# A transformer layer on one core: the sixteen transposes of a head's probabilities in one stretch, every other step

## What is computed

```python
q = split_heads(x @ wq + bq)            # 8 heads of 48 features
k = split_heads(x @ wk + bk)
v = split_heads(x @ wv + bv)
scores = jnp.einsum('bhqd,bhkd->bhqk', q, k) * scaling
scores = scores + attn_bias[:, None, :, :]          # adj
attn = jax.nn.softmax(scores, axis=-1)
ctx = jnp.einsum('bhij,bhjd->bhid', attn, v)
ctx = ctx.transpose(0, 2, 1, 3).reshape(b, n, d)
attn_out = ctx @ wo + bo
x = _rmsnorm(x + attn_out, alpha1, gamma1)
ff = jax.nn.silu(x @ w1 + b1) @ w2 + b2
x = _rmsnorm(x + ff, alpha2, gamma2)
# outside: layernorm(x_in + x)
```

## Time and profile before

| | us |
|---|---|
| median of the timed runs | 2019.77 |
| profiled execution, its own time | 2022.79 |
| its span | 2021.0 |
| PE busy in the span | 1951.2 |
| DVE busy in the span | 1457.0 |
| ACT busy in the span | 1231.1 |
| POOL busy in the span | 1007.5 |

### The profile page before, as it was taken

The page is one execution under the profiler, slowest core; times in us unless marked ns, Lnnn a source line. Parts: engine busy times, 40 slices in busy tenths (PEclk is TensorE's granted clock), DMA queues, the critical chain, the costliest instruction groups (busy, mean ns, idle before and its releaser), DMA issues. The chain is left out here.

```text
span 2021.0 us, 37267 instructions
## 1 busy us (share of the span) xinstructions
PE 1951.2 (97%) x10336; PEld 1696.9 (84%) x10336; DVE 1457.0 (72%) x3022; ACT 1231.1 (61%) x2408; POOL 1007.5 (50%) x1005
## 2 busy tenths in 40 slices
PE   6999999999999999999996999999999999999998
PEld 5887878888788878888775899999999999999997
DVE  5898899888898898988994555655555555555644
ACT  4887788877887788878874444444433443444332
POOL 3444444443444444443453666555556665555643
PEclk8999999999999999999997999999999999999999
DMA  6444544456444544456434222222111222222011
GB/s 204 117 125 121 164 125 128 125 139 164 110 124 125 159 130 134 119 137 164 111 89 157 83 75 78 78 78 78 66 55 43 72 76 78 78 78 78 16 40 39
DMA packets 114581, 210.12 MB, mean 104 GB/s; under 512 B 18160, under 2 KB 46576, under 8 KB 114544
## 3 DMA queue, kind: packets, MB, share of 16 engines
q1 hardware_dynamic: 114544, 209.67, 35.6%
HBM read 96.35 MB, written 37.75 MB: 66 GB/s over the span
## 5 line engine op out<-in xcount | busy, mean ns | idle before, releaser
L376 POOL TENSOR_SCALAR probs<-probs,inv_sum 128x512 f32<-128x512 f32 x256 | 401.9, 1570 | 515.7 <-DVE inv_sum L545 514.2
L444 ACT ACTIVATE probs<-probs,neg_max 128x512 f32<-128x512 f32 x512 | 364.6, 715 | 79.6 <-DVE neg_max L539 79.1
L531 DVE CUSTOM_DVE_ANT_0 probs<-ps_s,adj_s 128x512 f32<-128x512 f32 x480 | 309.6, 681 | 46.1 <-DMA adj_s<-in_adj 42.2
L557 DVE TENSOR_TENSOR pT_lo<-ps_t,pT_hi 128x1024 fp32r<-128x1024 f32 x256 | 312.0, 1219 | 27.5 <-ACT pT_hi L452 26.7
L452 ACT ACTIVATE pT_hi<-ps_t 128x1024 fp32r<-128x1024 f32 x256 | 261.4, 1021 | 88.7 <-PE ps_t L674 86.5
L1132 DVE TENSOR_TENSOR h_lo<-hidden,h_hi 128x512 fp32r<-128x512 f32 x192 | 168.5, 879 | 172.5 <-ACT h_hi L1038 172.0
L674 PEld LDWEIGHTS ps_t<-ident,probs 128*128 128x128 f32 x2048 | 240.2, 141 | 36.3 <-DVE probs L551 2.4
L674 PE MATMUL ps_t<-ident,probs 128*128 128x128 f32 x2048 | 266.8, 273 | 1.5 <-DVE probs L551 1.5
L1247 PE MATMUL ps_y<-w_hi,h_hi 128*128 128x384 f32 x768 | 257.9, 336 | 0.0
L1247 PE MATMUL ps_y<-w_hi,h_lo 128*128 128x384 f32 x768 | 256.6, 334 | 0.0
L1247 PE MATMUL ps_y<-w_lo,h_hi 128*128 128x384 f32 x768 | 256.6, 334 | 0.0
(11 more groups left out here) (104 smaller groups left out, 4071.4 us busy)
## 6 DMA issues: line engine op xcount, KB each, us to landing
q_both<-stage_q SPq DMA_DIRECT2D x192, 192.0 KB, 3.7
ctx_dram<-ctx_stage SPq DMA_DIRECT2D x256, 96.0 KB, 2.0
k_hl<-stage_k SPq DMA_DIRECT2D x192, 96.0 KB, 2.4
adj_s<-in_adj SPq DMA_DIRECT2D x32, 512.0 KB, 3.9
xT_raw<-in_xT SPq DMA_DIRECT2D x16, 768.0 KB, 4.8
ctx_a<-ctx_dram SPq DMA_DIRECT2D x16, 768.0 KB, 4.6
ctx_b<-ctx_dram SPq DMA_DIRECT2D x16, 768.0 KB, 6.1
x<-in_x SPq DMA_DIRECT2D x16, 768.0 KB, 6.5
```

What stands on the lines that cost most here:

```text
L376: pool.tensor_scalar(probs[:, at, :], probs[:, at, :], inv_sum[:, at:at + 1], None, ALU.mult).then_inc(probs_ready[1], 1)
L444: nc.scalar.activation(probs[:, at, :], probs[:, at, :], ACT.Exp, bias=neg_max[:, at:at + 1], accum_out=row_sum[:, at:at + 1])\
L531: nc.vector.tensor_tensor_reduce(out=probs[:, at, :], in0=ps_s[qt % 2][:, :], in1=rows, scale=1.0, scalar=-BIG, op0=ALU.add, op1=ALU.max, ...
L557: nc.vector.tensor_tensor(pT_lo[:, h % 2, s, :, :].rearrange("p q k i -> p (q k i)"), ps_t[pair][:, :, :].rearrange("p q n -> p (q n)"), p ...
```

## The change

`transpose_probs`, `pT_high` and `pT_low` are no longer called once in each step for the pair of the step. They are called twice in the odd steps, for pair 0 and pair 1 of the head, and in the even steps not at all. Nothing else is edited; tiles, waits and counts of instructions stay as they were.

```diff
--- before.py
+++ after.py
@@ ACT, batch(b) @@
                 for p in range(PAIRS):
-                    pT_high(b, p // 2, p % 2)
+                    for pair in (0, 1) if p % 2 else ():
+                        pT_high(b, p // 2, pair)
                     for of, h, pair in pairs_of(b, p + AHEAD):
                         exponent(of, h, 2 * pair)
                         exponent(of, h, 2 * pair + 1)
@@ DVE, batch(b) @@
                     for step, kind, t in steps_of(p - 1, b, "qk"):
                         project_lo(batch_of(step, b), kind, t, shared_bank(step))
-                    pT_low(b, p // 2, p % 2)
+                    for pair in (0, 1) if p % 2 else ():
+                        pT_low(b, p // 2, pair)
                     for pair in pairs_of(b, p + AHEAD - 1):
                         normalise(*pair)
@@ PE, batch(b) @@
                         scores(of, h, 2 * pair)
                         scores(of, h, 2 * pair + 1)
-                    transpose_probs(b, p // 2, p % 2)
+                    for pair in (0, 1) if p % 2 else ():
+                        transpose_probs(b, p // 2, pair)
                     for of, h, _ in context_at(b, p):
```

## The result

The changed kernel takes 2091.26 us (median of 4 runs, 2090.21 to 2092.55) against 2019.65 us before. The ratio is 1.0356, with a 95% interval of 1.0343 to 1.0368: 3.6% slower, 72 us. Forecast was slower, 2068 us, with a range of 2044 to 2094. So the direction held, the range held with 3 us to spare at its upper end, and 48 of the 72 us were forecast.

A forecast was written before the change was run, and what follows sets the result against it. PE was taken as the limit, with DVE 7.3 us a batch behind in attention. Loop terms summed to +3.0 us a batch, 45 in fifteen, plus 1 for the last: +46, set at 2068 us, range 2044 to 2094.

The forecast's parts named there:

- Changes between transposes and matmuls, 0: On PE, 128 stretches disappear: taken as 0 gain, at the most 1.3 us.
- The new wait and the loop through it: Odd-step logits on DVE wait for PE's transposes, some 0.7 us; loop 7.64 us with a projection, 6.97 without; chance 0.60.
- ACT in the q loops, 0.27: After a q projection the first pT_hi is ready after DVE comes for it: about 0.27 us lost, loop 7.91.
- rival 2: ACT binds in every projection loop: five loops lose 1.2 us more a batch, 18 in all, 2086 us; chance 0.15.
- 9 to 11: Attention loop between these odd steps: 7.64 us instead of 7.50, +0.14 a batch.
- 3 to 5: Attention loop without a projection between these odd steps: 6.97 us instead of 5.38, +1.59 a batch.
- 7 to 9, +0.10: Attention loop between these odd steps, 7.50 us before: 0.10 us longer a batch.
- The adj rows, +1.30: SP's transfers of q1 start later, so adj rows land 1.30 us later: steps 11 to 15 take 17.50 instead of 16.20.
- Step 1, +0.30: PE's v1 needs the context bank ACT stages behind two pT_hi: +0.3 us a batch, bounds -0.3 and +0.9.
- PE's granted clock stays at 1.00: PE keeps its higher clock level, 2.4 GHz, through the waits; a fall would mean the prediction is wrong.
- First and last batch: Start as before; each of fifteen batches +3.0 us, the last, with hardly any projections and held by DVE, +1.
- The blocked normalise: Even-step DVE normalise waits for POOL's whole 1.57 us; 30 us more, 2098 us; chance 0.03.

The follow-up runs named there:

- the first experiment: Changed kernel, but in odd steps TensorE does pair 0's eight transposes ahead of the step's scores, pair 1's behind them; 2052.00 us, 1.0154 of before.
- the run with the second half later: Changed kernel, but VectorE does pT_low of pair 1 one step later, in the next even step; 2078.18 us, 1.0287 of before.
- the one with the adj edit: Changed kernel, but SyncE queues the load of adj pair 1 ahead of the q1 projection's eight transfers; 2072.60 us, 1.0263 of before.
- the last run: Changed kernel with scores and logits two pairs ahead instead of three, and adj loads one step later (steps 12 and 13); 2048.70 us, 1.0140 of before.
- the run with the second half later and the adj edit: Changed kernel with pT_low of pair 1 in the next even step and adj pair 1 loaded ahead of q1's transfers; 2016.88 us, 0.9993 of before.
- the last two runs: Changed kernel with pair 1's pT_low a step later and adj pair 1 before q1's transfers, 2016.88 us; with scores two ahead, adj loads a step later, 2048.70 us.

## Why the prediction was right in direction and short in size

- **Changes between transposes and matmuls, 0**: right. The sixteen take 1.91 us, the same 0.11 each, and no gain shows.
- **The new wait and the loop through it**: right in the middle loops, and confirmed by the runs that remove it (first and last) and by the one that shortens what is behind it. The wait itself came out at 1.2 us on average (150.4 us in 126 times) and not at some 0.7. The size of the loop was 7.91 and not 7.64. The row that closes it shows two hops that I had too small. After a wait PE's first score pair takes 0.34 us to its second matmul (561.00 - 560.66), since its weight load had to wait as well and is no longer hidden, so the transposes start at S + 1.18 and not 1.08. And from the end of the eighth transpose (561.84 + 1.04 = 562.88) to the logits (563.05) are 0.17 us, where I took 0.04.
- **ACT in the q loops, 0.27**: wrong as a cause. (Its terms as written add up to about 0.2.) `pT_low` waits 1.8 us for `pT_hi` in the whole kernel; the wait comes up only where that for the transposes is gone, as in the first experiment. So rival 2 is out here, though its 2086 is nearer than 2068. That the q loops came out at the 7.91 of the forecast is luck: the two hops happen to be as large; the k loop (9 to 11) came out at 7.90 as well, where I had 7.64. 3 to 5 (6.97, as forecast) is luck of the same kind: PE is not late at step 3, so its transposes start 0.92 us behind the first score and not 1.08, and the longer hop makes up for it.
- **7 to 9, +0.10**: mis-sized. I let PE hold this loop; DVE's loop of 7.91 holds it: +0.43. With 9 to 11 and 5 to 7 that is 0.7 us a batch, 11 us in 15.
- **The adj rows, +1.30**: right. It was 1.15 in this batch (17.35 - 16.20) and 1.35 in the median of the looped batches, and the edit that takes them out of the path gives 1.7 back, as the loops say.
- **Step 1, +0.30**: 0.32.
- **"PE's granted clock stays at 1.00"**: the step that failed, and one that the prediction itself named as a sign of being wrong. The clock fell eight times, for 8 to 10 us. I had reasoned from today's waits being of this length, by the one of 0.99 us in the rows. They were not: the waits at step 15, before at most 1.3 us but for one of 1.77, now were 1.4 to 2.2, and one of 1.35 was new at step 5. The trace of the kernel before already had a fall, behind that wait of 1.77 us, outside the period that I had read. No rival had the clock in it.
- **First and last batch**: mis-sized. By the sum they are 3.0 and 1; the two came out at some 6.
- **The blocked normalise** (rival 4): it did not happen, but not for the reason I gave; see below.

So the range held in part because it was wide: 54 us came from the mechanism that was forecast where the sum had 42 for the same 14 batches, and 8 to 10 from a clock that was to stay at 1.00.

## What to carry to other kernels

Where an instruction waits on an engine with an order, add up the loop from its release to the next time the other engine needs its product, with everything queued between; a move that adds no work can still set the pace when two engines are as near each other as here (PE 63.5, DVE 57.4 of 64.7 us). Before a stretch is made longer, ask which buffer is freed at its end and who stands behind that wait. And look first at a queue whose transfers are in front of a load that someone waits for: here that was worth 1.2%, more than any order of the transposes.

## What the runs showed that was not expected

**DVE and POOL do take turns.** A normalise of DVE alone takes 0.48 us. Rows of the kernel before had 0.84 beside POOL's 1.57, and I read that as speaking against an exclusive lock. But DVE had come last in POOL's time: POOL's ends at 658.53 (656.96 + 1.57) and DVE's at 658.80, 0.27 later. Another pair of before, with less overlap, has the same distance: POOL ends at 600.75, DVE at 601.03.

```profile
599.18 1.57 POOL L376 TENSOR_SCALAR probs<-probs,inv_sum 128x512 f32<-128x512 f32 x1 [2.06 <-DVE inv_sum L545]
...
600.44 0.59 DVE L551 TENSOR_SCALAR probs<-probs,inv_sum 128x512 f32<-128x512 f32 x1
```

In the changed kernel DVE comes 0.11 us before POOL in the even steps, and now POOL is the longer one:

```profile
561.35 0.49 DVE L552 TENSOR_SCALAR probs<-probs,inv_sum 128x512 f32<-128x512 f32 x1
...
561.46 1.82 POOL L376 TENSOR_SCALAR probs<-probs,inv_sum 128x512 f32<-128x512 f32 x1 [3.22 <-DVE inv_sum L546]
```

Over all 256, DVE's mean went from 606 to 483 ns and POOL's from 1570 to 1693. Who starts first keeps its time, and the other is late: DVE ends the same 0.27 to 0.28 us behind POOL whether it came early or late in POOL's time, and POOL takes 0.25 us longer behind DVE. The Trainium skill ("SBUF — State Buffer", section "SBUF: two separate sides") calls the port pair that the two share an exclusive lock, which whoever starts first has for the whole instruction. By the constant 0.27 to 0.28 us the traces agree. I had misread the row of 0.84 us, and guessed wrong who would be first.

**The clock falls behind short waits.** A granted clock of 0.50 followed waits of PE of 1.8 to 3.2 us (every batch but the last in the run with the second half later), of 1.8 to 2.2 us (four of fourteen at step 15 of the changed kernel) and of 1.35 us (step 5: three of fourteen in the changed kernel, eight of fourteen in the one with the adj edit). Waits of up to 1.1 us brought none in the looped batches: 1.1 in thirteen batches of the run with pair 0 ahead, 1.06 in each batch of the last run, 0.75 in the run with the second half later and the adj edit. The stretch of sixteen isn't needed for it, as the fall in the kernel before shows, nor is it enough, as the last two runs show. The same wait in the same place brings a fall in some batches and not in others, so its cost is a share and not a sum to be worked out; no run here shows what decides.
